# Decoder block on one core: dividing the cross-attention after the values instead of before

## The reference, cut to what matters

```python
def _L0_xattn_ref(query, key, value, Wq, Wk, Wv, Wo):
    Q = _split_heads(query @ Wq.T); K = _split_heads(key @ Wk.T); V = _split_heads(value @ Wv.T)
    scores = jnp.einsum('bhqd,bhkd->bhqk', Q, K) / jnp.sqrt(jnp.float32(D_K))
    scores = scores + causal[None, None, :, :]
    attn = jax.nn.softmax(scores, axis=-1)
    heads = jnp.einsum('bhqk,bhkd->bhqd', attn, V)
    return heads.transpose(0, 2, 1, 3).reshape(B, S, D) @ Wo.T

x = x + _L0_attn_ref(_layernorm(x), ...)
x = x + _L0_xattn_ref(_layernorm(x), ctx_1024, ctx_1024, ...)
x = x + _L0_ffn_ref(_layernorm(x), ...)
```

## Time and profile before

| | |
|---|---|
| three runs | 1148.42, 1150.33, 1150.6 us; median 1150.33 |
| profiled execution | 1150.6 us, its span 1150.6 us |
| TensorE busy | 975.8 us (85%) |
| VectorE busy | 788.8 us (69%) |
| ScalarE busy | 577.3 us (50%) |
| GpSimd busy | 227.7 us (20%) |
| mean granted clock of TensorE | 0.921 of full speed |

### The profile page before, as it was taken

The page is one execution under the profiler, slowest core; times in us unless marked ns, Lnnn a source line. Parts: engine busy times, 40 slices in busy tenths (PEclk is TensorE's granted clock), DMA queues, the critical chain, the costliest instruction groups (busy, mean ns, idle before and its releaser), DMA issues.

```text
span 1150.6 us, 22137 instructions
## 1 busy us (share of the span) xinstructions
PE 975.8 (85%) x9069; PEld 767.2 (67%) x9069; DVE 788.8 (69%) x1841; ACT 577.3 (50%) x1148; POOL 227.7 (20%) x220
## 2 busy tenths in 40 slices
PE   6656899969998799978999699987999689987687
PEld 5553688737785587846886487855787477864566
DVE  3256866687866967678667878678666867669444
ACT  4434755367534665357553565346652575445322
POOL 6001410035000520024100440014200341004100
PEclk9886999979998899979999799989999799997789
DMA  5300010000100010000100010000100000000000
GB/s 146 80 1 1 2 38 1 11 10 2 38 10 10 2 38 1 11 10 2 37 11 1 11 31 8 10 11 2 38 1 10 11 2 1 10 11 1 1 1 19
DMA packets 28902, 18.36 MB, mean 16 GB/s; under 512 B 7649, under 2 KB 27394, under 8 KB 28802
## 3 DMA queue, kind: packets, MB, share of 16 engines
q1 hardware_dynamic: 26914, 12.48, 4.2%
q0 software_dynamic: 1280, 4.20, 1.2%
q10 hardware_dynamic: 608, 0.27, 0.1%
HBM read 12.62 MB, written 4.19 MB: 15 GB/s over the span
## 4 chain that ended last, share of the span: by engine, by line
PE 62%; DVE 21%; ACT 10%; POOL 3%; issue 3%; SPq 1%; DMA 0%; DVEq 0%; POOLq 0%
PE banks L510 7%; PE banks L674 5%; PE banks L491 5%; PE banks L493 5%; PE banks L492 5%; PE banks L606 4%; PE banks L624 4%; ACT M L867 3%; PE banks L648 3%; DVE PXUT L1222 3%; DVE mx L1221 3%; PE banks L769 3%; PE banks L541 2%; DVE sil L1166 2%; PE banks L598 2%
## 5 line engine op out<-in xcount | busy, mean ns | idle before, releaser
L874 ACT ACTIVATE sil<-banks,b 128x512 f32<-128x512 f32 x144 | 99.5, 691 | 199.6 <-PE banks L493 197.2
L867 ACT COPY M<-banks 128x512 f32<-128x512 f32 x208 | 122.9, 609 | 90.3 <-PE banks L624 70.2
L1166 DVE SCALAR_TENSOR_TENSOR sil<-banks,b,sil 128x512 f32<-128x512 f32 x128 | 95.8, 749 | 93.6 <-ACT sil L874 91.8
L510 PEld LDWEIGHTS banks<-w,hT 128*128 128x128 f32 x1152 | 151.5, 194 | 12.5 <-issue 7.2
L510 PE MATMUL banks<-w,hT 128*128 128x128 f32 x1152 | 154.5, 277 | 1.4 <-DVE hT L1173 1.4
L389 POOL DMA_DIRECT2D out_x<-xn x16 | 12.9, 809 | 534.3 <-DVE xn L1179 534.3
L426 POOL TENSOR_TENSOR PXUT<-PXUT,rx 128x512 f32<-128x512 f32 x80 | 87.2, 1117 | 101.7 <-DVE rx L1235 101.7
L1173 DVE TENSOR_TENSOR hT<-sil,banks 128x512 f32<-128x512 f32 x128 | 87.9, 687 | 25.1 <-PE banks L500 21.3
L624 PE MATMUL banks<-ident,PXUT 128*128 128x128 f32 x384 | 61.9, 301 | 31.7 <-ACT M L867 28.2
L598 PE MATMUL banks<-maskb,pick 32*64 32x512 bf16 x512 | 46.4, 506 | 46.6 <-ACT PXUT L930 28.2
L674 PEld LDWEIGHTS banks<-pooled,A 128*128 128x128 f32 x512 | 66.1, 207 | 19.9 <-DVE pooled L1286 18.6
(11 more groups left out here) (199 smaller groups left out, 2067.2 us busy)
## 6 DMA issues: line engine op xcount, KB each, us to landing
xin<-in_x SPq DMA_DIRECT2D x8, 512.0 KB, 4.1
cin<-in_ctx SPq DMA_DIRECT2D x8, 512.0 KB, 5.3
out_x<-xn POOLq DMA_DIRECT2D x16, 256.0 KB, 2.8
KQ<-in_L_attn_Wqkv SPq DMA_DIRECT2D x3, 512.0 KB, 5.3
KQ<-in_L_ffn_We SPq DMA_DIRECT2D x2, 512.0 KB, 4.6
KQ<-in_L_attn_Wo SPq DMA_DIRECT2D x1, 512.0 KB, 8.0
w<-in_L_ffn_We SPq DMA_DIRECT2D x1, 512.0 KB
woM<-xwT SPq DMA_DIRECT2D x16, 8.0 KB, 1.8
```

The costliest lines, as they stand in the source:

```text
L510: mm(ps(name)[:, P * t:P * t + P], hT[:, k % 2, P * t:P * t + P], w2[:, pair[k], :], start=(n == 0 and t == 0), stop=False, skip_group_che ...
L867: cp(dst, ps(name)[:] if src is None else src).then_inc(ready, 1)
L874: nc.scalar.activation(sil[:, k % 2, :], ps(f"H1_{k}")[:], ACT.Silu, bias=b1[:, pair[k]:pair[k] + 1]).then_inc(sil_ready, 1)
L1166: V.scalar_tensor_tensor(sil[:, k % 2, :], ps(f"H3_{k}")[:], b3[:, p:p + 1], sil[:, k % 2, :], ALU.add, ALU.mult).then_inc(hid_ready, 1)
```

## The change

All four tiles of a unit get the maximum and the subtraction on VectorE; the exponential of every tile is one ScalarE instruction in SBUF. The sums over the keys, the inversion of them and GpSimd's multiplications are gone: the tile is turned over undivided. The values get a column of ones beside each head's 8 columns (`Vx`, 18 columns for two sequences), so that the product with the values also gives the sum. In `values` the stationary operand is now the turned tile (64 columns of it) and the moving one the 18 columns of `Vx`, 32 products per unit. VectorE inverts the sums in PSUM and multiplies (`normalise_O`); the result has tokens as rows, so TensorE turns it over (`turn_O`), ScalarE copies it out (`O_moved`), and `project` uses the output weights as they are. `woM` and its 16 transfers are gone. `V_3` moves ahead of the next group's `xnT1` transposes.

The core of the diff (both engines' `both` functions follow the same order):

```diff
-    att = ["ctxT_0", "ctxT_1", "V_0", "V_1", "V_2", "xnT1_0", "xnT1_1", "V_3", "KT_0"]
+    att = ["ctxT_0", "ctxT_1", "V_0", "V_1", "V_2", "V_3", "xnT1_0", "xnT1_1", "KT_0"]
-             "yx": ([f"Yx_{u}" for u in range(UX)], 1)}
+             "yx": ([f"{kind}_{u}" for u in range(UX) for kind in ("OT", "Yx")], 1)}
...
-            sp.wait_ge(consts, 3)
-            sp.wait_ge(setup_cp, 2)
-            for s in range(2):
-                for b in range(2):
-                    for gq in range(4):
-                        sp.dma_start(woM[32 * gq + 16 * b:32 * gq + 16 * b + 16, s, b, :],
-                                     xwT[32 * gq + 16 * s:32 * gq + 16 * s + 16, 3, :]).then_inc(spread_wo, 16)
             sp.wait_ge(setup_cp, 4)
...
-                        nc.gpsimd.tensor_tensor(p, p, rx[:, u % 2, q].unsqueeze(2).to_broadcast([P, HALF, S]),
-                                                ALU.mult).then_inc(pn_ready, 1)
...
+                    pe.wait_ge(pr_ready, XS * g + k + 1)
...
-                for j in range(4):
-                    for q in range(XQ):
-                        rr = slice(32 * q, 32 * q + 32)
-                        last = mm(ps(name)[rr, P * j:P * j + P],
-                                  Vb[:, 2 * u + j // 2, 2 * q + j % 2, :, :].rearrange("p a c -> p (a c)"),
-                                  pT[:, (XQ * u + q) % PT, j, :], start=True, stop=True, tile_position=(0, 32 * q))
+                w = 2 * (XC + 1)
+                for t in range(2):
+                    for j in range(XH // 2):
+                        for r in range(2):
+                            o0 = w * (XH // 2) * t + w * j
+                            last = mm(ps(name)[64 * r:64 * r + 64, o0:o0 + w],
+                                      pT[:, (XQ * u + j // 2) % PT, 2 * t + j % 2, 64 * r:64 * r + 64],
+                                      Vx[:, 4 * u + 2 * t + r, j, :], start=True, stop=True)
...
+            def turn_O(g, u):
+
+                name = f"OT_{u}"
+                wait_free(pe, g, name)
+                pe.wait_ge(On_ready, UX * g + u + 1)
                 for t in range(2):
+                    last = turn_over(ps(name)[:, P * t:P * t + P], On[:, u % 2, t, :], ident[:])
+                last.then_inc(fulled(name), 1)
...
                         if u >= 3:
-                            project(g, u - 3)
+                            turn_O(g, u - 3)
                         if u >= 2:
                             values(g, u - 2)
+                        if u >= 3:
+                            project(g, u - 3)
...
-                if q == 0:
-                    act.wait_ge(mx_ready, UX * g + u + 1)
-                    for h in range(HALF):
-                        last = nc.scalar.activation(p[:, h, :], ps(f"S_{k}")[:, S * h:S * h + S], ACT.Exp,
-                                                    bias=mx[:, 0, h:h + 1])
-                    last.then_inc(pr_ready, 1)
-                else:
-                    act.wait_ge(dx_ready, 3 * UX * g + 3 * u + q)
-                    nc.scalar.activation(p, p, ACT.Exp).then_inc(pr_ready, 1)
+                act.wait_ge(dx_ready, XS * g + k + 1)
+                nc.scalar.activation(p, p, ACT.Exp).then_inc(pr_ready, 1)
...
+                    link(V.tensor_reduce(mx[:, q], sv, AX, ALU.max))
+                    V.tensor_tensor(pr[k % PR], sv, mx[:, q].unsqueeze(2).to_broadcast([P, HALF, S]),
+                                    ALU.subtract).then_inc(dx_ready, 1)
+
+            def normalise_O(g, u):
+
+                wait_full(dve, g, f"OL_{u}")
+                w = XC + 1
+                ov = ps(f"OL_{u}")[:, 0:2 * XH * w].rearrange("p (h c) -> p h c", c=w)
+                link(V.reciprocal(rx[:], ov[:, :, XC]))
+                V.tensor_tensor(On[:, u % 2].rearrange("p t (h c) -> p (t h) c", c=XC), ov[:, :, 0:XC],
+                                rx[:].unsqueeze(2).to_broadcast([P, 2 * XH, XC]), ALU.mult).then_inc(On_ready, 1)
...
             def both(e, g):
-                links["a"] = links["e"] = 0
-                if e is not None:
-                    inverses(e, UX - 1, "e")
-                    normalise_x(e)
+                if e is not None:
+                    normalise_O(e, UX - 3)
+                    add_x(e, UX - 4)
                     add_x(e, UX - 3)
                     for u in range(UX - 2):
                         stats_e(e, u)
+                    normalise_O(e, UX - 2)
...
                     add_x(e, UX - 2)
                     stats_e(e, UX - 2)
+                    normalise_O(e, UX - 1)
                 if g is not None:
                     apply("a", xin, xn, rstd_ready, 2 * g + 1, xn_ready)
```

More of the change, by code:

```diff
@@ L37, in decoder_block @@
     UX = T // 2
-    BY_DVE = (XQ * UX - 4, XQ * UX - 3)
-    BY_POOL = [k for k in range(XQ * UX) if k not in BY_DVE]
+    XS = XQ * UX
     E, EG, EI = 16, 4, 64
@@ L177, in decoder_block @@
         pT = M[:].rearrange("p a b h -> p (a b h)").rearrange("p (k j q) -> p k j q", k=PT, q=P)
-        On = KQ[:, 7, :].rearrange("p (a q) -> p a q", a=2)
+        On, OnT = [KQ[:, 7, 512 * k:512 * k + 512].rearrange("p (a t d) -> p a t d", a=2, d=D) for k in range(2)]
         g1 = sb("g1", [P, T])
@@ L273, in wait_free @@
                 pe.wait_ge(out_ready, CHUNKS * g)
-            elif ring == "att" and k % 2 == 0:
-                pe.wait_ge(pr_ready, XQ * UX * g)
+            elif ring == "att":
+                pe.wait_ge(dx_ready, XS * g)
         def wait_full(eng, g, name):
@@ L418, in both @@
                     store(e, 1)
-                if g is not None:
-                    for k in range(XQ * UX):
-                        u, q = k // XQ, k % XQ
-                        if k in BY_DVE:
-                            continue
-                        pool.wait_ge(rx_ready, 2 * UX * g + k // 2 + 1)
-                        p = pr[k % PR]
-                        nc.gpsimd.tensor_tensor(p, p, rx[:, u % 2, q].unsqueeze(2).to_broadcast([P, HALF, S]),
-                                                ALU.mult).then_inc(pn_ready, 1)
             run(pool, both)
@@ L642, in project @@
                 wait_free(pe, g, name)
-                pe.wait_ge(On_ready, UX * g + u + 1)
+                pe.wait_ge(OT_ready, UX * g + u + 1)
                 for t in range(2):
-                    for s in range(2):
-                        for r in range(2):
-                            c0 = P * (2 * t + s) + 64 * r
-                            last = mm(ps(name)[64 * r:64 * r + 64, P * t:P * t + P], On[:, u % 2, c0:c0 + 64],
-                                      woM[:, s, r, :], start=(s == 0), stop=(s == 1))
+                    last = mm(ps(name)[:, P * t:P * t + P], OnT[:, u % 2, t, :], xwT[:, 3, :], start=True, stop=True)
                 last.then_inc(fulled(name), 1)
@@ L684, in both @@
                     turn(e, UX - 2, (0, 1))
+                    turn_O(e, UX - 3)
+                    turn(e, UX - 2, (2, 3))
                     project(e, UX - 3)
-                    turn(e, UX - 2, (2, 3))
                 if g is not None:
@@ L692, in both @@
                     turn(e, UX - 1)
-                    project(e, UX - 2)
+                    turn_O(e, UX - 2)
                 if g is not None:
@@ L699, in both @@
                     values_of(g, 2)
+                if e is not None:
+                    turn_O(e, UX - 1)
+                if g is not None:
+                    values_of(g, 3)
                 if e is not None:
@@ L705, in both @@
                     four(g, "xnT1_1", xn, 1)
-                    values_of(g, 3)
                     keys_of(g, 0)
@@ L942, in both @@
                     PT_moved(e, XQ * (UX - 2))
+                    PT_moved(e, XQ * (UX - 2) + 1)
                     O_moved(e, UX - 3)
-                    for q in range(1, XQ):
-                        PT_moved(e, XQ * (UX - 2) + q)
+                    PT_moved(e, XQ * (UX - 2) + 2)
+                    PT_moved(e, XQ * (UX - 2) + 3)
                 if g is not None:
@@ L1029, in both @@
                                 PT_moved(g, XQ * (u - 2) + q)
-                            if q == 0 and u >= 3:
-                                O_moved(g, u - 3)
                             exp_x(g, XQ * u + q)
+                        if u >= 3:
+                            O_moved(g, u - 3)
             run(act, both)
@@ L1048, in _, with link @@
             V.tensor_reduce(plane[:], planes[:], AX, ALU.add).then_inc(plane_ready, 1)
-            links = {"a": 0, "e": 0}
-            def link(ins, g, kind="a"):
-                links[kind] += 1
-                signal, per = (vec_a, LINKS_A) if kind == "a" else (vec_e, LINKS_E)
-                ins.then_inc(signal, 1)
-                dve.wait_ge(signal, per * g + links[kind])
+            links = [0]
+            def link(ins, *_):
+                links[0] += 1
+                ins.then_inc(vec_step, 1)
+                dve.wait_ge(vec_step, links[0])
```

79 lines of the change are left out of this document (23 added, 56 removed).

## The result

| | before | after |
|---|---|---|
| median of five runs each | 1150.33 us (1148.42 to 1153.4) | 1192.36 us (1190.06 to 1199.84) |
| ratio, 95% interval | | 1.0376 [1.0349, 1.0403] |
| profiled execution | 1150.6 us, span 1150.6 | 1199.84 us, span 1198.1 |
| TensorE busy | 975.8 us | 1031.2 us |
| VectorE busy | 788.8 us | 731.8 us |

A forecast was written before the change was run, and what follows sets the result against it. TensorE was taken to hold most of the chain, with VectorE filling the loop's windows. 1150.6 + 23.1 (seven groups) + 1.0 (last group) - 9.3 (start) = 1165.4, forecast 1165 us; range 1148 to 1179.

The forecast's parts named there:

- The loop: First maximum to last subtraction: VectorE's units and TensorE's refills add up, 29.3 us, 2.4 more than before.
- rival 1: Loop: clock stays up, each refill 1.3 us less; two refills give 1144 us; chance of two or more 0.10.
- `values` and the division: Each unit: `values` 64 instructions in 1.9 us against 1.1 before; inversion 0.35 and product 0.42 us on VectorE.
- rival 2: `values`: the 18 columns are cheap, 1.0 us each, 22 us off, 1143 us; chance 0.05.
- rival 3: `values`: loads of the two halves go one after the other, 3.6 us each, +41, 1206 us; chance 0.07.
- The tail: After the loop: TensorE nearly packed, 13.9 us plus 0.8 of waits; `moments` at 51.1 against 47.8, 3.3 later per group.
- The prediction's rival on the clock: Same as rival 1: full clock in the loop makes refills shorter and the kernel faster; chance 0.10.
- its signs of being wrong: Full clock in the loop, refill overlapping subtractions, `values` far from 1.9 us, or first `moments` still at 44 us.
- The last group: Final group: no next group fills its tail's gaps; +1.0 us, taken between nothing and 3.3.
- The start: Before the first `moments`: without 16 transfers the loads end earlier; -9.3 us, bounds 0 and -9.8.
- Rival 4: Start gives nothing back, since another wait holds the first split or `pooled`: 1174 us; chance 0.08.

The follow-up runs named there:

- tile0: Changed kernel with tile 0 of each unit as before: VectorE takes only its maximum, ScalarE forms the exponential in eight pieces; 1171.48 us, ratio 1.0184.
- loopbusy: Changed kernel with never-read dummy products in TensorE's wait for unit 0's division and in the refills from unit 1 on; 1158.12 us, ratio 1.0090.
- pairs: Changed kernel with each unit's score banks refilled two at a time instead of as a set of four; 1138.77 us, ratio 0.9902.
- before_pairs: Kernel before, with woM's 16 transfers behind the experts' loads and score banks refilled two at a time; 1118.15 us, ratio 0.9739.
- busy: Changed kernel with one never-read 512-column product per group in TensorE's wait for unit 0's division; 1166.88 us, ratio 1.0159.
- ctx_in_wait: Changed kernel with the next group's eight context transposes moved into TensorE's wait for unit 0's division; 1171.38 us, ratio 1.0174.
- early: Changed kernel with unit 0's division ahead of the third tile of unit 3 in VectorE's order; 1192.91 us, ratio 1.0357.
- the control behind the wait: Changed kernel with one never-read 512-column product per group behind, not in, TensorE's wait for unit 0's division; 1182.35 us, ratio 1.0280.
- before_wo_later: Kernel before, with only woM's 16 transfers put behind the experts' weight loads in SyncE's program; 1138.26 us, ratio 0.9899.
- pairs_split: `pairs` with `turn(0)` in two halves, each ahead of its half of the refill of unit 3; 1195.12 us, ratio 1.0402.

## Why the prediction missed

**The loop: right.** 29.3 us were forecast from first maximum to last subtraction, 30.1 came; units and refills add up, with VectorE waiting for TensorE's scores. A refill costs 2.87 us each time (in the first, 0.6 of it goes to another instruction of VectorE) where 2.5 to 2.8 were forecast, a unit 5.4 where 5.3 were. The loop of this group stood at the lower clock for 13.7 us, as long as before (that the windows above read 0.78 and 0.70 against 0.50 and 0.76 comes from where they begin), and the granted clock over its three refills is 0.50 to 0.51, so rival 1 did not come. Its price was right: where a refill ran at full clock, in `tile0` and `loopbusy`, the wait fell from 2.87 us to 1.59. `pairs` shows the mechanism, `tile0` the share of the extra subtraction, and `before_pairs` that the refill was covered in the kernel before.

**`values` and the division: right.** `values` takes 2.00 to 2.05 us at full clock where 1.9 was forecast; the inversion 0.35 and the product 0.42 are as forecast. So neither rival 2 (1.0 us) nor rival 3 (the loads one after the other, 3.6 us) came; the 2.94 of `values(1)` is the clock's, as `busy` shows. The Trainium skill ("TensorE: Matmul & The Clock Gate", section "Part 3: Packing small matmuls — row/col tiling") would let these loads overlap with products only in different row groups. Here all rows are used, and 64 loads with their products take 2.0 us, not 3.6, so the trace does not agree.

**The tail: the step that failed.** The prediction said "From here TensorE has its work nearly packed" and priced that work by rows at full clock. The tail, from the last subtraction to the `moments`, was to be 21.8 us (29.3 to 51.1) and took 25.1. From the start of `values(1)` to the `moments` it had 20.7 us (30.4 to 51.1). At full clock that price holds: in `busy` it is 388.75 to 409.71, 21.0 us. In the changed kernel it is 399.65 to 423.54, 23.9 us. Packed is what TensorE was (8.00 of 8.00 us), but at 0.57 of its clock. The term that is missing, some 3 us per group, is what `busy` (25 us) and `ctx_in_wait` (21 us) take back with one edit at the gap ahead of it. The prediction's rival on the clock looked only the other way, to a faster loop, and none of its signs of being wrong named the clock in the tail. The further 1.0 us per group arose before `values(1)`, which started at 31.4 instead of 30.4: the loop's 0.8 and a wait for the division, with ScalarE's last copy as late (`early`).

That the lower clock is the cost is shown by the rows, at equal instructions. What brings it to just this place is not settled. Filling the gap removed it in seven groups of seven in `busy` and in `ctx_in_wait`, in five in `loopbusy`; dividing earlier left a gap of about the same size and the clock as it was; but the control behind the wait removed it in five groups of seven with the gap open, and in `pairs` it was gone in five of seven with a gap of 0.97 us. What TensorE does in the loop ahead may have a part in it; no run here separates that. The Trainium skill (the same page, section "Part 1: The HAM clock gate (the "warmup" mystery)") says that the point at which the clock rises varies from run to run. The trace agrees in that it varies between the groups of one execution, from 38.4 to 39.5 us after zero in the tails of the changed kernel.

**The last group: too small.** It was forecast 1.0 us longer from its first maximum to the end, a figure taken between two bounds; in the traces it is 130.6 against 123.5 us, 7.1 longer, and 127.5 in `busy`. It has the same serial loop, and the same gap in its tail.

**The start: right in its mechanism.** -9.3 was forecast, and the transfers alone are worth 12.4 us in `before_wo_later` (1150.69 to 1138.26). In the profiled execution of after it reads less, 7.4 us to the first zero: `moments` at 38.41 and 9.04 us long, since stretches at the start stood at the lower clock there. Rival 4, a start that gives nothing, is out.

**From `moments` to the next first maximum** nothing was forecast; it fell from 85.3 to 84.3 us per group, and a short stretch at the lower clock at 418 us of the trace of before has no counterpart in after. All together, for the profiled executions: seven groups from zero to `moments` +54.8 (forecast +23.1), seven times from there to the next zero -7.0 (0), the last group +7.1 (+1.0), the start to the first zero -7.4 (-9.3); the sum is +47.5, the difference of the spans.

## What to carry to other kernels

Work that is removed from a waiting engine may have been the cover of something else: here the sums on VectorE hid the refill of a set of banks, and without them the refill of the whole set stood on the path until it was split. Price work that follows a wait of TensorE at both levels of its clock, not only at that of the rows before, and carry the difference in the range; here it was some 3 us per group, 24 us in eight, and the range ended 14 us above the forecast. If a short gap of an engine at the end of a loop is followed by slower products, try useful work in the gap (21 us in `ctx_in_wait`), and read from the trace whether another wait takes its place, as in `early`, and where the clock now falls, as in `pairs_split`.

## What was not expected of the hardware

TensorE stayed at its lower clock while it was busy without a break: 8.00 of 8.00 us at a granted clock of 0.50 in two windows running (`pairs_split`), and 0.57 over 8 us in the changed kernel. And one product of 1.02 us per group, with no use, made the kernel 25 us faster, since the 8.0 us of work behind it (2.94, 1.23, 1.91 and 1.92) took 4.8.
